# Graph attention kernel: a fourth octet of node rows taken straight from x, table fills moved behind the last chunk, and every fourth edge window fetched row by row by ScalarE

## The reference

```python
h = x @ w_lin + b_lin
msg = h[edge_src]
counts = segment_sum(ones, edge_dst, n);  starts = cumsum(counts) - counts
pos = arange(e) - starts[edge_dst]
dense = zeros((n, 32, d)).at[edge_dst, pos].set(msg, mode='drop')
mask  = zeros((n, 32), bool).at[edge_dst, pos].set(True, mode='drop')
xb = _mab(dense, dense, enc..., mask)          # self attention, out proj, residual, relu ff
xp = relu(xb @ pma_lin_w + pma_lin_b)
p  = _mab(seed, xp, pma..., mask)              # one seed row attends to the 32 slots
dd = _mab(p, p, dec...)                        # one row
out = layernorm(x + relu(nan_to_num(dd)))
```

## Time and profile before

| | us |
|---|---|
| median of three runs | 4050.09 |
| the profiled execution | 4049.53 |
| its span, first to last instruction | 4047.7 |
| PE busy | 3126.2 (77%) |
| DVE busy | 3055.1 (75%) |
| POOL busy | 3000.5 (74%) |
| ACT busy | 1664.2 (41%) |
| granted PE clock, mean | 0.916 of full |

### The profile page before, as it was taken

The page is one execution under the profiler, slowest core; times in us unless marked ns, Lnnn a source line. Parts: engine busy times, 40 slices in busy tenths (PEclk is TensorE's granted clock), DMA queues, the critical chain, the costliest instruction groups (busy, mean ns, idle before and its releaser), DMA issues.

```text
span 4047.7 us, 105796 instructions
## 1 busy us (share of the span) xinstructions
PE 3126.2 (77%) x30784; PEld 2002.5 (49%) x30784; DVE 3055.1 (75%) x7166; ACT 1664.2 (41%) x3002; POOL 3000.5 (74%) x3168
## 2 busy tenths in 40 slices
PE   7777777777777777877777777777777877877777
PEld 4545454544454445545455454455444554544444
DVE  6777777777777777777777777777777777777876
ACT  3444444444434434444444444444444444444443
POOL 6777777777777777777777777777777777777772
PEclk8899999899999999999999999899998998999888
DMA  6333333333333333333333333333333333333331
GB/s 213 89 89 88 90 90 88 89 88 90 90 88 89 90 88 89 88 90 89 88 89 90 88 89 87 90 89 88 89 89 88 90 87 90 90 88 89 87 108 35
DMA packets 182788, 368.53 MB, mean 91 GB/s; under 512 B 64029, under 2 KB 116549, under 8 KB 182165
## 3 DMA queue, kind: packets, MB, share of 16 engines
q0 software_dynamic: 152048, 315.92, 29.4%
q1 hardware_dynamic: 29797, 45.03, 3.6%
q10 hardware_dynamic: 320, 0.10, 0.0%
HBM read 348.01 MB, written 16.32 MB: 90 GB/s over the span
## 4 chain that ended last, share of the span: by engine, by line
POOL 70%; issue 23%; PE 3%; DVE 1%; DMA 1%; POOLq 1%; ACT 0%; SPq 0%; DVEq 0%
POOL gathered L615 69%; DMA gathered<-node_table,idx 1%; PE ps L809 1%; POOL windows L572 1%; PE ps L732 1%; PE ps L782 1%; PE ps L683 0%; PE ps L720 0%; POOLq L128 0%; DVE xb L1257 0%; POOLq L130 0%; PE ps L837 0%; DVE windows L1086 0%; DVE gathered L1104 0%; DVE probs_diag L1330 0%
## 5 line engine op out<-in xcount | busy, mean ns | idle before, releaser
L615 POOL DMA_INDIRECT gathered<-node_table,idx x3101 | 2941.2, 948 | 951.1 <-issue 938.5
L720 PE MATMUL ps<-ident,gathered 128*128 128x128 f32 x3128 | 601.7, 323 | 615.6 <-DMA gathered<-node_table,idx 611.4
L720 PEld LDWEIGHTS ps<-ident,gathered 128*128 128x128 f32 x3128 | 497.2, 204 | 966.3 <-issue 807.8
L892 ACT ACTIVATE qT<-ps,cols 128x512 f32<-128x512 f32 x391 | 268.7, 687 | 1080.9 <-PE ps L720 1073.2
L1257 DVE SCALAR_TENSOR_TENSOR xb<-ps,cols,h 128x512 f32<-128x512 f32 x391 | 292.6, 748 | 519.2 <-PE ps L782 518.4
L846 ACT ACTIVATE h_apart<-ps 64x512 f32<-64x512 f32 x782 | 462.2, 591 | 452.8 <-PE ps L720 434.2
L1330 DVE STREAM_TRANSPOSE probs_diag<-probs 32x512 f32<-32x512 f32 x784 | 548.9, 700 | 18.4
L782 PE MATMUL ps<-h,ff_diag 128*128 128x512 f32 x782 | 501.4, 729 | 40.5 <-DVE h L1213 40.4
L732 PE MATMUL ps<-probs_diag,gathered 128*64 128x128 f32 x6256 | 452.3, 288 | 81.6 <-issue 80.2
L732 PEld LDWEIGHTS ps<-probs_diag,gathered 128*64 128x64 f32 x6256 | 365.1, 168 | 250.0 <-issue 232.0
L809 PE MATMUL ps<-xb,pma_diag 128*128 128x512 f32 x782 | 459.6, 670 | 33.6 <-DVE xb L1257 28.9
(11 more groups left out here) (203 smaller groups left out, 3368.0 us busy)
## 6 DMA issues: line engine op xcount, KB each, us to landing
windows<-win_table SPq DMA_DIRECT2D x8960, 2.8 KB
gathered<-node_table,idx POOLq DMA_INDIRECT x3101
node_table<-gathered SPq DMA_DIRECT2D x24, 384.0 KB, 3.1
out_rows<-rows SPq DMA_DIRECT2D x5, 416.0 KB
win_table<-in_dst SPq DMA_DIRECT2D x1, 1716.0 KB
win_table<-in_src SPq DMA_DIRECT2D x1, 1716.0 KB
rows<-in_x SPq DMA_DIRECT2D x2, 640.0 KB, 5.4
rows<-in_x SPq DMA_DIRECT2D x1, 768.0 KB, 7.4
```

The costliest lines, as they stand in the source:

```text
L615: pool.indirect_dma_start(out=gathered[:, s.slot(0, RING), t * ROW:(t + 1) * ROW], out_offset=None, in_=table, in_offset=bass.IndirectOffs ...
L720: mm = pe.transpose(ps[:, bank, p * P:(p + 1) * P], gathered[:, s.slot(0, RING), lo:lo + 2 * ROW - 2:3], ident[:, :])
L892: nc.scalar.activation(qT[:, s.slot(0, 4), :], ps[:, B_Q, :], ACT.Identity, bias=c_("q_b", P)).then_inc(q_sb, 1)
```

## The change

`FILLED` goes from 3 to 4, so octets 0 to 3 come from rows of x: 32 gathers of x rows instead of 24, 8 fills instead of 6. `FILL_AFTER` puts five fills behind chunk 24 and leaves three for after the preparation; none stands between chunks. The samples are laid out as 50 partitions x 25, their diagonal is written in two parts, and PE's first `spread` waits for the first part only. `search(0)` stands behind item 1 instead of item 3. `wlin` and `sample_i` move into memory that is used later.

The window of every fourth iteration, from iteration 8 on, is fetched by ACT: `act_rows_of` on DVE (step -21) makes the byte offsets and turns them, `fetch_rows` on ACT loads 32 of them into registers at a time and issues one DMA per row. The 128 rows are laid over 39 places in 13 steps (-19 to -7, three places a step: ahead of the copy to `xp_rows`, ahead of `qT`, ahead of `h_apart`), 3 or 4 rows a place. POOL keeps the window gather of iteration 4 alone. The core of the diff:

```diff
-SAMPLE_TILES = 10
+SAMPLE_TILES = 25
-FILLED = 3
+FILLED = 4
+AT_ACT_ROWS = -21
+ACT_FIRST = 2 * PERIOD // 4
+ACT_STEPS = range(-19, -6)
-    FILL_AFTER = (16, 19, 24, 24)
+    FILL_AFTER = (24, 24, 24, 24, 24)
-        wlin = sb("wlin", [P, D])
+        wlin = h2[:, 0, 0:D]
...
 # POOL
-                if s.has_iteration(AT_STRETCH) and s.slot(AT_STRETCH, PERIOD) == 0 and (s.looped or s.at >= 16 + AT_STRETCH):
+                if not s.looped and s.at == 4 * DIRECT + AT_STRETCH:
...
 # PE
+            pe.wait_ge(samples_sb, 2)
             spread(512, 1024)
 # ACT
+            PLACES = [(r, i) for r in ACT_STEPS for i in range(3)]
+            QUAD_PLACES = [9, 10, 10, 10]
+            JOBS = [(q, DEG * i // n, DEG * (i + 1) // n) for q, n in enumerate(QUAD_PLACES) for i in range(n)]
+            def fetch_rows(s, place):
+                for (r, i), (q, lo, hi) in zip(PLACES, JOBS):
+                    if i != place or s.slot(r, PERIOD) or not (
+                            s.looped or 4 * ACT_FIRST <= s.at - r < 4 * ITS):
+                        continue
+                    if q == 0 and lo == 0:
+                        wait_apart(act, act_turned_ready, s.period(r) - 1, act_passed)
+                        wait_apart(act, idx_ready, s.iteration(r) - 3, act_passed)
+                        if not s.looped:
+                            act.wait_ge(table_in, 64)
+                    if lo == 0:
+                        _, loaded[0] = nc.values_load_multi_w_load_instructions(
+                            odd_turned[DEG * q:DEG * q + 1, 3, :], engines=(mybir.EngineType.Activation,), ...)
+                    for j in range(lo, hi):
+                        act.dma_start(windows[DEG * q + j:DEG * q + j + 1, 0, 0:2 * WIN].bitcast(U8),
+                                      win_bytes[:, bass.ds(loaded[0][j], WIN_BYTES)]).then_inc(act_in[q], 16)
...
+                fetch_rows(s, 0)
                 if s.has(L_BACK):
                     ...
                     copy(xp_rows[:, s.slot(L_BACK, RING), :], ps[:, B_HX, :]).then_inc(back_sb, 1)
+                fetch_rows(s, 1)
                 if s.has(0):
                     ...
                     nc.scalar.activation(qT[:, s.slot(0, 4), :], ps[:, B_Q, :], ACT.Identity, bias=c_("q_b", P)
                                          ).then_inc(q_sb, 1)
+                fetch_rows(s, 2)
+                if s.has(0):
                     act.wait_ge(h_ps, s.octet(-1))
 # DVE
-            V.tensor_tensor(sample_diag[:, :, :], ...)
+            for lo, hi in ((0, 12), (12, SAMPLE_TILES)):
+                V.tensor_tensor(sample_diag[:, lo:hi, :], ...).then_inc(samples_sb, 1)
...
-                count_rows(u, at, u)
+                count_rows(u, at, u + (at == OCTS_PER_IT - 1))
+            def act_rows_of(s):
+                u = s.iteration(AT_ACT_ROWS)
+                n = s.period(AT_ACT_ROWS) - 1
+                count_rows(u, 0, u - 1)
+                V.tensor_scalar(win_idx[:, 0:1], win_row[:, 0:1], -1.0, float(WIN_BYTES), ALU.add, ALU.mult
+                                ).then_inc(act_idx_ok, 1)
+                wait_apart(dve, act_idx_ok, n, dve_passed)
+                V.transpose(odd_turned[:, 3, :], win_idx[:, 0:1].broadcast_to((P, DEG))).then_inc(act_turned_ready, 1)
...
-                    dve.wait_ge(win_in[0], s.period(AT_SEARCH) * 16 + 32)
+                    for q in range(QUADS):
+                        dve.wait_ge(act_in[q], s.period(AT_SEARCH) * (16 * DEG) - 16 * DEG)
-                if i == 3:
+                if i == 1:
                     search(0)
```

More of the change, by code:

```diff
@@ L196, in gnn_kernel @@
         win_table = nc.dram_tensor("win_table", (SAMPLES, 2 * WIN), I32).ap()
+        win_bytes = win_table.rearrange("r n -> (r n)").unsqueeze(0).bitcast(U8)
         table = nc.dram_tensor("node_table", (N, ROW), F32).ap()
@@ L273, in gnn_kernel @@
         samples = sb("samples", [P, SAMPLES])
-        sample_i = sb("sample_i", [SAMPLE_ROWS, SAMPLE_TILES], I32)
         sample_f = lnv[0:SAMPLE_ROWS, 0, 0:SAMPLE_TILES]
@@ L279, in gnn_kernel @@
         flags = [sb(f"flags{i}", [P, n], BF16) for i, n in enumerate((SAMPLES, WIN, WIN))]
-        odd_turned = sb("odd_turned", [P, 3, DEG], I32)
+        odd_turned = sb("odd_turned", [P, 4, DEG], I32)
         win_row = sb("win_row", [P, 4])
@@ L285, in gnn_kernel @@
         windows = sb("windows", [P, 4, 2 * WIN + DEG], I32)
+        sample_i = windows[0:SAMPLE_ROWS, 2, 0:SAMPLE_TILES]
         node_i = windows[:, 3, 0:ITS]
@@ L347, in gnn_kernel @@
         odd_in = [[sem(f"odd_in{b}{q}") for q in range(QUADS)] for b in range(3)]
+        act_in = [sem(f"act_in{q}") for q in range(QUADS)]
+        act_idx_ok = sem("act_idx_ok")
+        act_turned_ready = sem("act_turned_ready")
         odd_idx_ok = sem("odd_idx_ok")
@@ L416, in gnn_kernel @@
         pe_passed, pool_passed, dve_passed = sem("pe_passed"), sem("pool_passed"), sem("dve_passed")
-        sp_passed = sem("sp_passed")
+        sp_passed, act_passed = sem("sp_passed"), sem("act_passed")
         block = ctx.enter_context(nc.Block())
@@ L522, in _ @@
                              ).then_inc(table_in, 16)
-            win_bytes = win_table.rearrange("r n -> (r n)").unsqueeze(0).bitcast(U8)
             def odd_rows(b, count):
@@ L870, in _ @@
             rows_even(AHEAD, len(ITEMS))
+            PLACES = [(r, i) for r in ACT_STEPS for i in range(3)]
+            QUAD_PLACES = [9, 10, 10, 10]
+            JOBS = [(q, DEG * i // n, DEG * (i + 1) // n) for q, n in enumerate(QUAD_PLACES) for i in range(n)]
+            loaded = [None]
+            def fetch_rows(s, place):
[10 more added lines that the diff above has]
+                        _, loaded[0] = nc.values_load_multi_w_load_instructions(
+                            odd_turned[DEG * q:DEG * q + 1, 3, :], engines=(mybir.EngineType.Activation,), min_val=0,
+                            max_val=(SAMPLES - 1) * WIN_BYTES,
+                            skip_runtime_bounds_check_because="a count of the samples, less one, in bytes of a row")
+                    for j in range(lo, hi):
+                        act.dma_start(windows[DEG * q + j:DEG * q + j + 1, 0, 0:2 * WIN].bitcast(U8),
+                                      win_bytes[:, bass.ds(loaded[0][j], WIN_BYTES)]).then_inc(act_in[q], 16)
             def step(s):
@@ L941, in _ @@
             link(V.tensor_copy(sample_f[:, :], sample_i[:, :]))
[L942 to L946, removed]
+            for lo, hi in ((0, 12), (12, SAMPLE_TILES)):
+                V.tensor_tensor(sample_diag[:, lo:hi, :],
+                                ident[0:SAMPLE_ROWS, 0:SAMPLE_ROWS].unsqueeze(1).broadcast_to(
+                                    (SAMPLE_ROWS, hi - lo, SAMPLE_ROWS)),
+                                sample_f[:, lo:hi].unsqueeze(2).broadcast_to((SAMPLE_ROWS, hi - lo, SAMPLE_ROWS)),
+                                ALU.mult).then_inc(samples_sb, 1)
             V.memset(consts[:, :], 0.0)
@@ L1057, in landed @@
                         dve.wait_ge(odd_in[at - 1][q], s.period(AT_SEARCH) * (16 * DEG))
-                else:
-                    dve.wait_ge(win_in[0], s.period(AT_SEARCH) * 16 + 32)
+                elif not s.looped and u < ACT_FIRST:
+                    dve.wait_ge(win_in[0], 32 + 16)
+                else:
+                    for q in range(QUADS):
+                        dve.wait_ge(act_in[q], s.period(AT_SEARCH) * (16 * DEG) - 16 * DEG)
                 return at
@@ L1323, in step @@
                     index_of(searched[0], s.slot(AT_SHIFT, PERIOD) // OCTS_PER_IT)
-                if s.has_iteration(AT_ROWS) and (s.looped or s.at >= 4 * DIRECT + AT_ROWS):
+                if s.has_iteration(AT_ROWS) and (s.slot(AT_ROWS, PERIOD) or s.at == 4 * DIRECT + AT_ROWS) and (s.looped or s.at >= 4 * DIRECT + AT_ROWS):
                     rows_of(s)
+                if s.has_iteration(AT_ACT_ROWS) and s.slot(AT_ACT_ROWS, PERIOD) == 0 and (
+                        s.looped or s.at >= 4 * ACT_FIRST + AT_ACT_ROWS):
+                    act_rows_of(s)
             def to_diagonal(s, pr, first, last):
```

## The result

The change made the kernel faster, by what was forecast: 4013.45 us (median of four runs, 4012.69 to 4015.3) against 4050.88 us (four runs, 4048.23 to 4055.37), a ratio of 0.9911 [0.9899, 0.9922]. Forecast were 4013.5. The profiled execution took 4014.11 us, its span is 4012.3 (4047.7 before).

What follows compares the result with a forecast made beforehand. POOL, issuing indirect DMAs without a break, was taken as the bound: 68.07 us start + 3095 x 1.2533 + 64.1 tail = 4011.2 span, plus 1.8 outside and 0.6 for the median, forecast 4013.5 us, range 4008 to 4022.

Steps and rivals of the forecast that it cites:

- POOL's count: POOL's indirect DMAs: 31 fewer (8 table gathers, 23 windows) at 1.2533 us each, 38.85 us less.
- Start of the x gathers: Earlier search and split diagonal move POOL's first x gather 1.23 + 0.71 us earlier, to 28.10 us.
- The table's cover: Stored table ready near 62.8 us, before POOL's x gathers end at 68.07: 5.3 us of cover, cost nothing.
- rival C: At the start, POOL waits for the table or for PE at octet 8, losing the octet's 7.6 us: 4021; chance 0.06.
- First steps: More fills around the preparation make octet 0 attended 2.8 to 4 us later; cost nothing, 4 us once if cover is gone.
- ACT: Row fetch adds 49.1 us of issue a period; some 13 stick out, within PE's 23.8 us to spare; POOL loses nothing.
- Rival A: Steps -19 to -7: ACT's issue falls on the path and sets the pace, 582 us more, 4595; chance 0.07.
- middle case: ACT's issue costs 25 us a period on the path, about half of the added issue: about 4040 us.
- The branch: ACT's pause of up to 5.42 us behind its loop branch; if doubled, 18 of 23.8 us used, still hidden.
- SP: SP's row work stays, rows 0.317 us apart; its wait for DVE goes from 7.8 to 6.6 us a period.
- rival B: ACT's issue slows SP's row issue, making SP the pace: 4328 us at 0.16 us per row; chance 0.10.
- Rival D: Another engine was as late as POOL all along, so time stays near 4050; no chance of its own apart from A.

Runs made afterwards that it cites:

- e9: Windows change alone (old start), with a second 4-byte indirect DMA behind every table gather: 7885.48 us, 28.1 less than the kernel before loaded the same way.
- e8: Whole changed kernel, with a second 4-byte indirect DMA behind every table gather: 7868.09 us, 45.5 less than the kernel before loaded the same way.
- e7: Kernel before, with a second 4-byte indirect DMA behind every table gather so that POOL is the pace: 7913.59 us.
- e10: New start alone (windows left on POOL), with a second 4-byte indirect DMA behind every table gather: 7899.34 us, 14.25 less than the kernel before loaded likewise.
- e11: Changed kernel run again unaltered, on a chip where the kernel before takes 4050 us: 4013.45 us, ratio 0.991 to before.
- e4: Changed kernel with the first two fills back behind chunks 16 and 19, on the slow chip: 6526.93 us, ratio 1.0161 to the kernel before.
- e12: Changed kernel with each ACT row fetched in two half-size DMAs (256 a period, not 128), on a 4050 us chip: 4368.92 us, ratio 1.0792 to before.
- e2: Changed kernel without ACT's row fetch (new start, windows left on POOL), on the slow chip: 6474.28 us, ratio 1.0077 to the kernel before.
- e1: Changed kernel with the old start (ACT's row fetch kept), on the slow chip: 6496.26 us against 6426.68 for the kernel before, ratio 1.0109.
- e6: Changed kernel with tiles 6 and 7 of each octet not gathered from the table, on the slow chip: 5678.75 us, ratio 0.8839 to the kernel before.

## Why the prediction was right, step by step

**POOL's count: right, and shown.** Nothing holds POOL; 31 DMAs x 1.2533 us. e9 measures the 23 windows by themselves and e8 the whole, in kernels where nobody but POOL can matter; the unaltered pair gives 35.4 us between the spans and 37.4 between the medians, where the sum had 36.5. That 4013.5 met 4013.45 so closely is luck: the span came out 1.1 us longer than the sum, and the median of the runs lay 0.7 below the profiled execution instead of 0.6 above it.

**Start of the x gathers: right.** 28.04 us, 28.10 forecast. Both terms of the move can be read in the timeline of the kernel after: PE's spread begins at 7.95 instead of 8.63, behind the first of the two halves, and the indices are turned out at the end of a search that began earlier.

```profile
7.12 1.52 DVE L978 TENSOR_TENSOR xp_rows<-ident,lnv 50x600 f32<-50x600 f32 x2
...
7.95 2.07 PE L634 MATMUL ps<-xp_rows,pool_part 50*128 50x512 f32 x2 [7.95 <-DVE xp_rows L978]
...
60.66 0.36 DVE L1153 COPY gathered<-ps 128x192 f32<-128x192 f32 x1 [0.71 <-DMA node_table<-gathered]
...
61.46 1.11 SPq L519 DMA_DIRECT2D node_table<-gathered  x1
```

POOL's next DMA was at 68.00 (68.07 forecast). It is the first of `gather_direct(3)`, though, not a table gather as my list of signs had it: that one is at 70.50. The count holds both, so the sum is untouched.

**The table's cover: right in sign, half in size.** I had it ready near 62.8 us, with 5.3 us to spare; it was ready by 65.5, with 2.5 to spare. The last rows above say why. Taking two fills from ahead of the last chunk was to bring it 2.8 us forward; its copy came only 0.94 us earlier (60.66 against 61.60), and it waited 0.71 us for an earlier store to land. In the first 66 us DVE and ACT now wait 4.0 us for stores of the table, where they did not before: what the fills had filled was partly time in which the stores were late anyway. One pair of profiles doesn't even give the sign. With the old start the same copy stands at 61.60 (before) but at 59.0 in e7 and e9, with the new one at 60.66, 60.5 (e8), 60.0 (e10) and 60.0 (e11), and the table was ready at 65.6 (before), 63.8 and 63.7 with the old start, by 65.5 (the kernel after, e8) and 64.3 (e10, e11) with the new one. So no run shows that the new places of the fills make the table earlier. With a cover of 2.5 us, rival C was nearer than its 0.06 says. Whether the old places of the fills would have made POOL wait was asked in e4, which ran in the wrong regime: it stays open on the faster chip.

**First steps: hidden, as said, by less.** The first turn of octet 0 is at 80.1 us (75.4 before), 4.7 us later where I had 2.8 to 4. PE frees octet 0's slot at 99 us (its last matmul of line 738), 13 us before POOL wants it; before, that margin was 26. Half of it went: 4.7 us by the later octet, and 7.6 (10.0 - 2.4) because POOL reaches octet 8 sooner, now that octet 3 no longer stands ahead of it. My text named the first and not the second. POOL's waits for PE still sum to only 1.5 us.

**ACT: hidden, and cheaper than I had it.** This is the term that was mis-sized. PE's wait for gathers fell by 159 us, 6.9 a period, where 14 were forecast (452 us left, not 290). e11, the same kernel once more, has 440.2 left. 1.25 of the 6.9 is POOL's shorter period, which leaves 5.7, and some 1.3 of these are PE's own, at the loop's branch (below). So ACT's 49.1 us of issue cost PE an estimated 4 to 6 us a period and not 13. The timeline of ACT in a stretch with a load and the loop's branch tells the reason:

```profile
1934.90 1.06 ACTq L900 DMA_DIRECT2D windows<-win_table  x3
1936.07 0.60 ACT L852 ACTIVATE xp_rows<-ps 128x512 f32<-128x512 f32 x1 [4.41 <-issue]
1936.15 1.15 ACTq L900 DMA_DIRECT2D windows<-win_table  x4
...
1970.47 0.27 ACT L852 ACTIVATE pooledT<-ps 64x128 f32<-64x128 f32 x1 [7.74 <-PE ps L841]
```

The four rows at 1936.15 go out from 0.08 us after the start of the activation at 1936.07, beside it: the busy time of ACT is free for issue too, not only its idle time. I had counted idle time alone. What still shows is the place with the load, 4.41 us ahead of `xp_rows`. e12 finds the limit. Its second DMA of a row comes 0.37 us behind the first (823.65 and 824.02 us in its trace), so doubling adds about 47 us of issue a period. PE's wait for gathers falls from 440.2 us (e11) to 6.5, 18.9 a period, and 15.5 us stand on top: 34 of the 47 are on the path. Not all of the 34 need be the issue itself: PE is also busy 144 us longer than in e11 (3264.2 against 3120.5), 6.2 a period, at a mean granted clock of 0.887 of full against 0.919. So a first 49 us cost 4 to 6 and the next 47 cost up to 34. Rival A's break-even (25.4 us a period on PE) was a fair condition, but its premise, that the issue waits until the activation before it is through, is false; and a middle case interpolated between nothing and all, which I had put at 4040, has no meaning with a limit of this kind.

**The branch: hidden, but misread.** The pause of 5.42 us ahead of `pooledT` is 7.74 us in the kernel after. Over the first 21 branches its median is 6.3 us before (5.3 to 6.9) and 7.7 after. But it is not ACT's: in both rows it ends with a matmul of PE. For most of it PE stands at its own branch instruction (duration ns min/median/max; before, then after):

```profile
L430 PEldq COMPARE_BRANCH  x22: 83/3732/4387, 369.9 to 3760.0; - x22
...
L437 PEldq COMPARE_BRANCH  x22: 83/4983/5519, 362.0 to 3725.3; - x22
```

PE's longer branch comes with the new start and not with ACT's rows: the median is 3.6 us in e7 and e9, which have the old start, and 4.9 to 5.0 in e8 and e10, and of these four only e8 and e9 have ACT's rows. Why PE's branch is longer there, with the body of its loop unaltered, stays open. ACT's own pause, from its branch to the next instruction of its loop, had a median of 0.26 us with 225 instructions in a turn of the loop and has one of 2.96 us with 489. It is over before PE's. POOL shows the same step: 0.27 us with 170 instructions (kernel after), 2.6 us with 318 (e8). That agrees with the rule of the Trainium skill that the prediction names (Runtime: NRT & Kernel Launch, "Instruction fetch mechanics"), that a jump out of the window has to fetch. The prediction was wrong to conclude that ACT's pause stays: before, ACT paid for no such jump.

A load of 2.1 us starts on ACT together with `pooledT`, so the first turns of PE around this branch stand 18.4 us apart, 15.3 before, and are back at their distance from the gathers some six octets later. It was never late enough for POOL.

**SP: right, and rival B is out.** SP's issues have the same median beside ACT's stream, 225 ns, also beside the doubled one, and ACT's stay at 213 to 214. From start to start, between its loads, SP's rows are 318 ns apart at the median before, after and in e12 (means 327, 328 and 330). SP's wait for DVE is 136.9 us in 22 waits, 6.2 each, 6.6 forecast. B asked for 64 ns per row of ACT; there is none. The Trainium skill's sentence on the page DMA: Bandwidth & Descriptors ("Queues, rings and completion order"), that the two have no descriptor generator of their own, has no price at this rate (about 220 ns of issue every 320). Against that, B's 0.10 of chance was too much.

**What the forecast did not know** is that it holds only where the kernel before takes 4050 us. Where the kernel before takes 6426 us, each half of the change is slower, by 70 and 48 us. Rival D describes that chip, not this one: there other engines are late all along, and the sum over POOL's DMAs says nothing.

## What to carry to other kernels

When one engine issues without a break, the time is its start plus count times interval plus its tail: count what leaves that engine, read its first and last instruction, and check that each other engine's wait for it is longer than what you load onto it. Here ACT's DMA issues hid beside its busy time as well as its idle time, but up to a limit beyond which most of them were paid; leave distance to such a limit, since the position is seen in the waits (452 of 611 us left here) long before it is seen in the time. Read who ends a pause before you put it down to the engine that stands still: the 5.42 us behind ACT's branch were PE's. And a time is worth only what the profile's regime is worth: look first whether the pacing engine paces on the chip at hand.

## What was not expected of the hardware

- An indirect DMA costs POOL the same at 4 bytes per partition as for a row of the table: in e7 3101 of either kind took 945 and 946 ns, 1.2502 us apart.

```profile
L619 POOL DMA_INDIRECT gathered<-node_table,idx x3101 | 2932.5, 946 | 950.2 <-issue 944.4 <-DMA node_table<-gathered 5.3 <-PE ps L741 0.6
L624 POOL DMA_INDIRECT spare<-in_src,idx x3101 | 2931.4, 945 | 944.7 <-issue 943.5 <-PE ps L741 1.2
```

- One program takes 4050 us on one chip and 6426 us on another. The granted TensorE clock is lower there (0.76 of full in e2, 0.92 in the kernel after here), but e7 has 0.71 on the faster chip with POOL's intervals unaltered, so a low mean doesn't mark the slow chip. What does is that PE and SP issue single instructions over a microsecond apart in the same stretch, as the timeline of e2 shows. A move between registers on SP, at most 41 ns in the kernel before on the faster chip, took up to 1408 ns in e2:

```profile
L541 SPq MOVE windows<-win_table x8960: 1/29/1408, 202.5 to 6259.6; - x200
```

Its median stayed at 29 ns, so only some instructions are hit. What these engines wait for in such a stretch no profile shows, and since e1 to e6 all ran on the one chip, it is open whether it is the chip or its state at the time.
